# Retention stage of a fused network: head sums on column groups with channels on partitions, products in a buffer of their own, norm scaling on ScalarE, blocks unrolled

## What is computed

```python
def step(carry, xs):
    S, K = carry
    pq, pk, vt, bt, mt = xs        # elu(rope(q))+1, elu(rope(k))+1, v, beta, mix
    K = K * bt[..., None] + pk[:, :, None, :]
    S = S * bt[..., None, None] + pk[:, :, None, :, None] * vt[:, :, None, None, :]
    num = jnp.einsum('bhd,bhmdc->bhmc', pq, S)
    den = jnp.einsum('bhd,bhmd->bhm', pq, K) + EPS
    y = jnp.sum(num / den[..., None] * mt[..., None], axis=2)
    return ((S, K), y)
...
y = jnp.moveaxis(ys, 0, 1).reshape(b, t, H) @ Wout.T + bout
z = x + y                          # here x is the normed input of the stage
mu = z.mean(-1, keepdims=True)
var = ((z - mu) ** 2).mean(-1, keepdims=True)
return (z - mu) / jnp.sqrt(var + LN_EPS) * ln_g + ln_b
```

## Time and profile before

| what | value |
| --- | --- |
| time, median of 3 runs | 2612.34 us (2611.93 to 2614.21) |
| profiled execution, its own time | 2613.99 us |
| span in its trace | 2612.3 us |
| busy over the whole span | PE 84%, DVE 69%, ACT 37%, POOL 20% |
| retention stage in the trace | about 959.5 to 1376 us |
| mean granted TensorE clock, whole span | 0.87 |

### The profile page before, as it was taken

One profiled execution on the slowest core, in us unless ns is written; L12 is line 12 of the kernel. 1 busy time (PEld: TensorE's weight loads), 2 busy tenths in 40 slices (PEclk: granted clock), 3 DMA queues, 4 the chain that ended last, 5 costly groups with the idle time before them and its releaser, 6 DMA issues. The chain is left out here.

```text
span 2612.3 us, 39415 instructions
## 1 busy us (share of the span) xinstructions
PE 2200.8 (84%) x12850; PEld 1667.5 (64%) x12850; DVE 1804.5 (69%) x5506; ACT 967.5 (37%) x1477; POOL 521.4 (20%) x526
## 2 busy tenths in 40 slices
PE   3777589988799987677667997799989999997999
PEld 2555479876688864545556986455555555556888
DVE  4778678863277867987877886666666666646787
ACT  1223034431144431111103443255656565563443
POOL 0000010100010102322311001244343344421000
PEclk8878689996689996666658998799999999997999
DMA  2000010000000000000000000000000000000000
GB/s 83 3 3 3 2 43 0 0 1 0 0 1 1 1 34 1 1 0 0 0 0 1 0 0 1 1 1 1 1 1 1 1 1 1 1 1 5 9 9 13
DMA packets 13993, 14.90 MB, mean 6 GB/s; under 512 B 3924, under 2 KB 11669, under 8 KB 13334
## 3 DMA queue, kind: packets, MB, share of 16 engines
q1 hardware_dynamic: 13846, 13.11, 1.6%
HBM read 10.22 MB, written 2.88 MB: 5 GB/s over the span
## 5 line engine op out<-in xcount | busy, mean ns | idle before, releaser
L2095 DVE TENSOR_REDUCE soft_mx<-psum 128x1 f32<-128x512 f32 (+3 forms) x608 | 381.0, 659 | 226.5 <-PE psum L1973 132.5
L2016 ACT ACTIVATE soft_prob<-psum 128x1024 f32<-128x1024 f32 (+3 forms) x384 | 306.4, 813 | 217.7 <-PE psum L1904 214.7
L1969 PE MATMUL psum<-soft_own,soft_stack 128*128 128x512 f32 (+3 forms) x768 | 248.3, 384 | 26.8 <-DVE soft_mx L2095 24.4
L1904 PE MATMUL psum<-soft_stack,soft_own 128*128 128x512 f32 (+3 forms) x768 | 233.2, 387 | 1.1 <-ACT soft_prob L2016 0.7
L1904 PEld LDWEIGHTS psum<-soft_stack,soft_own 128*128 128x128 f32 x768 | 119.9, 191 | 142.0 <-issue 89.2
L1969 PEld LDWEIGHTS psum<-soft_own,soft_stack 128*128 128x128 f32 x768 | 142.6, 196 | 80.0 <-DVE soft_mx L2095 62.3
L1919 PE MATMUL psum<-soft_prob,soft_v_pad 128*32 128x512 f32 (+3 forms) x1536 | 164.5, 500 | 5.2 <-ACT soft_prob L2016 3.3
L982 DVE SCALAR_TENSOR_TENSOR x<-psum,ffn1b_cw,x 128x128 f32 (+1 forms) x512 | 144.1, 344 | 32.1 <-PE psum L869 23.1
L982 DVE SCALAR_TENSOR_TENSOR x<-psum,ffn1a_cw,x 128x128 f32 (+1 forms) x512 | 144.1, 344 | 32.0 <-PE psum L869 22.8
L982 DVE SCALAR_TENSOR_TENSOR x<-psum,ffn0b_cw,x 128x128 f32 (+1 forms) x512 | 144.1, 344 | 31.8 <-PE psum L869 22.8
L982 DVE SCALAR_TENSOR_TENSOR x<-psum,ffn0a_cw,x 128x128 f32 (+1 forms) x512 | 144.1, 344 | 31.5 <-PE psum L869 22.5
(11 more groups left out here) (440 smaller groups left out, 4367.8 us busy)
## 6 DMA issues: line engine op xcount, KB each, us to landing
s_ffn_w<-in_ffn_w SPq DMA_DIRECT2D x4, 1024.0 KB, 6.0
out_x<-x SPq DMA_DIRECT2D x8, 256.0 KB, 2.3
mamba_coef_dram<-mamba_out_coef SPq DMA_DIRECT2D x8, 96.0 KB, 1.6
s_ret_w<-in_ret_w SPq DMA_DIRECT2D x1, 640.0 KB
s_ret_cos<-in_ret_cos SPq DMA_DIRECT2D x1, 512.0 KB
s_ret_sin<-in_ret_sin SPq DMA_DIRECT2D x1, 512.0 KB
s_mamba_in<-in_mamba_in SPq DMA_DIRECT2D x1, 256.0 KB
s_soft_sel<-in_soft_sel SPq DMA_DIRECT2D x1, 256.0 KB
```

The source lines that it names most:

```text
L1904: ins = pe.matmul(e_ps[:, n % 2, j, low(n):BLK], own[:, u % 3, 2 * pair + j, kt * P:(kt + 1) * P], stack[:, u % HT, qb * BLK + low(n):(qb ...
L1969: ins = pe.matmul(per_head[:, n, :], stack[:, u % HT, i * P:(i + 1) * P], own[:, u % 3, g, half * BLK:half * BLK + width], start=(n == 0), ...
L2016: nc.scalar.activation(prob[:, done % PROBS, :, low(n):BLK], e_ps[:, n % 2, :, low(n):BLK], ACT.Exp, scale=float(HD) ** -0.5).then_inc(exp ...
L2095: nc.vector.tensor_reduce(mx[:, i, half, heads.start:heads.stop], bank[:, 0:width * len(heads)].rearrange("p (g k) -> p g k", k=width), AX ...
```

## The change

The stage's engine lists are rewritten. What differs:

- **Products.** `state` keeps its values, the ten products of a block go to a new buffer `prod` of five planes, all on DVE. The scans of a sequence's second block start from the last column of `state` itself; the carry copy is gone, and so are POOL's products.
- **Head sums.** The head selector is the stationary operand with 32 columns, the product streams. Four such matmuls take the four groups of 32 columns of the array (`tile_position`), and sums come out with channels or heads on partitions. Denominators: 4 matmuls of 128 columns; numerators: 4 of 512 columns, for each decay. The mixture logits are made in the same way.
- **Division.** ACT copies the denominators with the epsilon added and copies the numerators to SBUF. DVE inverts and multiplies by `mix` (`invert`). PE spreads the 128x128 quotients over channels (`spread`, 8 matmuls with a new constant), into the numerators' banks. DVE multiplies (`divide`), one iteration later than before. PE projects the two decays with accumulation, 8 matmuls; the transpose of `y`, its copy and the addition on DVE are gone.
- **Norms.** Both scalings move from DVE to ACT, which takes `rstd` as scale and `-mean*rstd` as bias. DVE negates the means, POOL multiplies them by `rstd`.
- **Ring.** Three PSUM banks in turn for ten products, the two decay projections among them. The order on every engine is new, and all eight blocks are written out.
- `res` keeps four blocks. A new 128x4x128 constant is loaded with the stage's other weights.

```diff
-POOL_STATES = ((1, 2), (1,))
 W_V, W_BETA = 4, 8
-RING = 8
+JOBS = (0, 1, 2, 3, W_BETA, W_BETA + 1, W_V, W_V + 1, W_V + 2, W_V + 3)
+RING_BANKS = 3
+KEPT = 4
...
+            def invert(q):
+                norm.invert(pool, q)
+                pool.wait_ge(norm.rstd_ready, q + 1)
+                nc.gpsimd.tensor_tensor(shift[:, :], norm.mv[:, :, 0], norm.rstd[:, :], ALU.mult).then_inc(shift_ready, 1)
-            def products(q, p, m):
-                pool.wait_ge(carried, DECAYS * q + m + 1)
-                for s in POOL_STATES[m]:
-                    st = state[:, m, s, :]
-                    ins = nc.gpsimd.tensor_tensor(st, st, phi[:, p, 0, :], ALU.mult)
-                ins.then_inc(prod_pool, 1)
...
             def sums(q, m):
-                for j in range(GT):
-                    cols = slice(j * P, (j + 1) * P)
-                    pe.matmul(den_ps[:, m, j, :], state[:, m, 0, cols], w["head_sel"][:, :], start=True, stop=True)
-                    for c in range(HD4):
-                        ins = pe.matmul(num_ps[:, m, j, c, :], state[:, m, 1 + c, cols], w["head_sel"][:, :],
+                pe.wait_ge(den_prod, n + 1)
+                if m == 0:
+                    pe.wait_ge(mix_tanh_done, min(q + 2, BLOCKS))
+                for j in range(GT):
+                    ins = pe.matmul(den_ps[RH * j:RH * (j + 1), m, :], w["head_sel"][:, :], prod[:, 0, j * P:(j + 1) * P],
+                                    start=True, stop=True, skip_group_check=True, tile_position=(0, RH * j))
+                ins.then_inc(den_ready, 1)
+                pe.wait_ge(num_prod, n + 1)
+                for c in range(HD4):
+                    ins = pe.matmul(num_ps[RH * c:RH * (c + 1), m, :], w["head_sel"][:, :], prod[:, 1 + c, :],
+                                    start=True, stop=True, skip_group_check=True, tile_position=(0, RH * c))
+                ins.then_inc(num_ready, 1)
+
+            def spread(q):
+                pe.wait_ge(rd_ready, q + 1)
+                for m in range(DECAYS):
+                    pe.wait_ge(num_copied, DECAYS * q + m + 1)
+                    for j in range(GT):
+                        ins = pe.matmul(num_ps[:, m, j * P:(j + 1) * P], w["spread"][:, j, :], rd[:, m, :],
                                         start=True, stop=True)
+                    ins.then_inc(spread_ready, 1)
...
+            def scale(q):
+                for j in range(GT):
+                    ins = nc.scalar.activation(norm.xn[:, j, :], x[:, q * GT + j, :], ACT.Identity,
+                                               scale=norm.rstd[:, j:j + 1], bias=shift[:, j:j + 1])
+                ins.then_inc(norm.xn_ready, 1)
...
+            for i in range(BLOCKS):
+                if i + 2 < BLOCKS:
+                    scale(i + 2)
+                if i + 1 < BLOCKS:
+                    decays(i + 1)
+                    mixture(i + 1)
+                    exponentials(i + 1)
+                copy_num(i, 0)
+                if i + 2 < BLOCKS:
+                    copy_x(i + 2)
+                if i:
+                    scale_z(i - 1)
+                copy_den(i)
+                copy_num(i, 1)
...
                 for s in range(STATES):
                     ins = nc.vector.tensor_tensor_scan(
                         state[:, m, s, :], beta[:, p, m, :], phi[:, p, 1, :] if s == 0 else kv[:, p, s - 1, :],
-                        0.0 if p == 0 else carry[:, m, s:s + 1], ALU.mult, ALU.add)
+                        state[:, m, s, BLK - 1:BLK] if p else 0.0, ALU.mult, ALU.add)
                 ins.then_inc(scanned, 1)
-                nc.vector.tensor_copy(carry[:, m, :], state[:, m, :, BLK - 1]).then_inc(carried, 1)
                 for s in range(STATES):
-                    if s in POOL_STATES[m]:
-                        continue
-                    st = state[:, m, s, :]
-                    ins = nc.vector.tensor_tensor(st, st, phi[:, p, 0, :], ALU.mult)
+                    ins = nc.vector.tensor_tensor(prod[:, s, :], state[:, m, s, :], phi[:, p, 0, :], ALU.mult)
+                    if s == 0:
+                        ins.then_inc(den_prod, 1)
+                ins.then_inc(num_prod, 1)
...
+            def invert(q):
+                dve.wait_ge(den_copied, q + 1)
+                nc.vector.reciprocal(rd[:, :, :], rd[:, :, :]).then_inc(inverted, 1)
+                dve.wait_ge(mix_ready, q + 1)
+                nc.vector.tensor_tensor(rd[:, :, :], rd[:, :, :], mix[:, q % 2, :, :], ALU.mult).then_inc(rd_ready, 1)
+            def divide(q):
+                for m in range(DECAYS):
+                    dve.wait_ge(spread_ready, DECAYS * q + m + 1)
+                    nc.vector.tensor_tensor(ym[:, m, :], num_ps[:, m, :], num[:, m, :], ALU.mult).then_inc(ym_ready, 1)
```

More of the change, by code:

```diff
@@ new lines, in project @@
+            def project(q):
+                pe.wait_ge(ym_ready, DECAYS * (q + 1))
+                if q:
+                    pe.wait_ge(z_ready, q)
+                for j in range(GT):
+                    for m in range(DECAYS):
+                        ins = pe.matmul(y_ps[:, j, :], ym[:, m, j * P:(j + 1) * P], w["out"][:, :],
+                                        start=(m == 0), stop=(m == DECAYS - 1))
+                ins.then_inc(y_ready, 1)
+            tokens(0)
+            ring(0, range(6))
@@ L1475, in _ @@
+            project(BLOCKS - 1)
         @block.scalar
@@ L1490, in sigmoids, with decays @@
+            def decays(a):
+                for i in range(DECAYS):
+                    act.wait_ge(ring_ready, len(JOBS) * a + 4 + i + 1)
+                    if a:
+                        act.wait_ge(beta_ready, a)
+                    nc.scalar.activation(th[:, i, :], ring_ps[:, (len(JOBS) * a + 4 + i) % RING_BANKS, :], ACT.Tanh,
+                                         bias=half_b[:, i:i + 1], scale=0.5).then_inc(tanh_done, 1)
                 act.wait_ge(tanh_done, DECAYS * (a + 1))
-                if not first:
-                    act.wait_ge(carried, DECAYS * (a - 1))
@@ new lines, in _ @@
+            statistics(0)
+            statistics(1)
+            rope(0)
+            features(0)
+            for i in range(BLOCKS):
+                if i + 2 < BLOCKS:
+                    statistics(i + 2)
+                if i + 1 < BLOCKS:
+                    rope(i + 1)
+                if i:
+                    divide(i - 1)
+                scans(i, 0)
+                if i:
+                    add_residual(i - 1)
+                if i + 1 < BLOCKS:
+                    features(i + 1)
+                scans(i, 1)
+                if i:
+                    finish(i - 1)
+                invert(i)
@@ L1682 @@
+            divide(BLOCKS - 1)
+            add_residual(BLOCKS - 1)
+            finish(BLOCKS - 1)
 HEADS, HD = 16, 8
```

429 lines of the change are left out of this document (192 added, 237 removed).

## The result

The changed kernel took 2530.89 us (median of 4 runs, 2529.36 to 2531.32), the kernel before beside it on the same chip 2613.28 us (4 runs, 2611.93 to 2614.66). The ratio is 0.9684, 95% interval 0.9667 to 0.97. The predicted time was 2526 us. Its profiled execution took 2530.77 us, with a span of 2529.0 us.

The account below looks back on a forecast made before the run. The bound was taken as a cycle in the retention stage: DVE's work plus its waits for PE. Work 280, waits 46 and gaps 6 gave 331 us against 416.5, -85.5, so 2526 us from 2612.34; range 2504 to 2554.

Parts of the forecast that it names:

- rival 5: DVE's products stay at 1.37 us because something other than POOL slowed them: +34, 2560; chance 0.04.
- Collisions: POOL's `keep` beside DVE's scans: two of 1.05 us for six blocks, 12.6 us; 13 in place of 7, +6.
- the fourth rope product behind the spreading: PE makes it after eight spreading matmuls, so DVE waits 2.8 us a block at 1.2 GHz, none at 2.4.
- `kv`: Fourth product waits for one of three PSUM banks: DVE waits 0.9 us a block at 1.2 GHz, none at 2.4.
- Features: PE's and ACT's chain ends at 23.1 us, DVE at 22.4: it waits 0.7 at 1.2 GHz, nothing at 2.4.
- No wait before the reciprocal: At `divide`, the denominators' sums and copy are hidden at both clock levels, so the 33.0 us wait goes.
- Rivals 3 and 4: Column groups run in series: +50, 2577, chance 0.06; with 1.2 GHz for the whole stage too: 2615, chance 0.03.
- The drain at a change of tiling mode: PE changes between full width and four column groups four times a block; softmax shows no gap there.
- ACT's scalings: Norm scalings as 8 ACT instructions of 128x128 a block, 0.39 us at most each, 3.1 us beside DVE's scans.
- A few us either way: The FFN following the retention stage starts at whichever clock level that stage left, shifting time by a few us.
- Rival 1: Lower clock throughout, as PE does fewer matmuls: waits rise by 11, start and end by 5, about 2545; chance 0.14.
- rival 2: Higher clock more often, or fewer collisions: the 22 us of steady waits vanish, 2506; chance 0.13.

Follow-up runs that it names:

- g1_dve_products: Kernel before, with all ten products of a block on DVE, still in place, and POOL's products and their waits gone: 2603.11 us, ratio 0.9959.
- h5_pool_products: Changed kernel with three of the ten products of a block back on POOL, still into the separate buffer: 2538.67 us, ratio 0.9723.
- h6_keep_late: Changed kernel with POOL's `keep` moved behind the power of z and held until the next block's `phi` is made: 2513.54 us, ratio 0.9639.
- h8_double_num: Changed kernel with the four numerator matmuls of each decay made twice, same values over themselves: 2521.79 us, ratio 0.9668.
- g3_unrolled: Kernel before, with the loop over the retention stage's four middle blocks written out, nothing else: 2622.9 us, ratio 1.0043.
- i2_pad: Changed kernel with 40 unused one-element memsets on DVE at the retention stage's start, moving later DVE code: 2512.22 us, ratio 0.9622.
- i1_all: Changed kernel with `keep` released by `phi`, fourth rope product between the two spreadings, and ACT's exponentials ahead of the mixture: 2506.5 us, ratio 0.9597.
- all three edits together: Kernel before, all products on DVE, norm scalings on ACT, head sums of three of four numerator columns left out: 2574.51 us, ratio 0.9858.
- h7_rope_between: Changed kernel with PE's fourth rope product put between the two decays' spreadings, not behind both: 2524.11 us, ratio 0.9671.

## Why the prediction was right, and where it missed

**Time and direction.** 2526 us was predicted, 2530.89 measured, inside the range of 2504 to 2554. The two errors of the sum have opposite signs: the stage came out at 324.5 us where 331 was predicted, 6.5 less, and the rest of the span at 2204.5 in place of 2195.8, 8.7 more where nothing was counted. So the span became 2529.0 in place of 2526.8. That these two nearly cancel is luck; the stage's own error, 2%, is the measure of the forecast.

**DVE's work, 280 us predicted, 277.2 measured.** Products 50.1 and 49.6, right; rival 5 (they stay slow) falls, and g1_dve_products and h5_pool_products show that POOL was the cause. The norm scalings left DVE, right. Collisions: twelve at 1.05, 12.6 us, were put on `keep`; h6_keep_late, which takes `keep` off the scans, gained 12.2. Right, and it was also cheap to remove.

**DVE's waits and gaps, 46 + 6 predicted, 47.3 measured.** By stretch: start 12 predicted and 37.20 - 24.84 = 12.4 measured; end 12 and 10.8; the steady part, 22 and the gaps of 6, came to 24.1. Inside the steady part the forecast had the largest item right, the fourth rope product behind the spreading (2.8 x 0.7 x 7 = 13.7, measured 13.6 with 1.2 of it at the start). `kv` was 7.3, 6.3 without the start, where 0.9 x 0.7 x 7 = 4.4 follows from the walk. Features were 3.4 and measured 1.7, at the start alone. The wait at `ym` was not in the walk: 6.1 us, of which 3.2 belong to the end. The share of the lower clock was taken over from before, 70%; the mean of 0.71 makes it 58%, but the spreading stood in the lower part: 3.78 us in six of eight blocks, where h8_double_num has 2.06 to 3.12. So the total of the steady waits came out nearly right from one item that was right, one too small, one too large and one that was missing.

**No wait before the reciprocal, numerators in 2.1 us at the lower level.** Right: none, and 1.94 us (1.93 or 1.94 in all sixteen sets). Rivals 3 and 4, which needed serial groups, fall. (The forecast says that weights and streams differ by group here as in softmax; here the four groups take the same head selector, and only the streams differ.) All sixteen sets ran at the lower level; of the higher one i1_all shows a single mixed case, 1.27 us.

**The drain at a change of tiling mode.** In h8_double_num the full-width spreading starts at 1163.17, before the modelled end of the groups' matmuls at 1163.24. As in the earlier trace rows, no gap is seen. The Trainium skill, TensorEngine Tiling (Array Packing), Tiling Modes, has a drain there; a cost of 0.2 us or more at this change should have shown as a gap, as far as the modelled end can be trusted.

**ACT's scalings, "0.39 us at most".** Mis-sized: 483 ns. Four of them in order take 1.65 us. DVE waits for them where nothing covers them: 3.2 us at the start of the stage (`n_stats` behind `n_xn`) and 3.1 at its end, each time together with POOL's power.

**"A few us either way" for the rest.** This is the step that missed. The few us came to 8.7, and the reason given, the clock level that the stage leaves to the following FFN, was not it: that FFN took 238.5 us where it took 239.4. The last FFN lost 7.1 us through the place of DVE's code; g3_unrolled and i2_pad show it from both sides. The trace of the kernel before has such pauses in the same place, 2.1 and 2.2 us, so they could have been a term. That all eight blocks are written out was costed at nothing; alone it is worth 0.4% to the worse. The other 3.8 us, in the stages ahead, are within what traces differ by.

**Slips of the working.** 280 + 46 + 6 is 332; 331 was taken. Rival 1's terms (11 and 5 on top of 2526) give 2542 where 2545 is written, and rival 2's give 2504, not 2506. Rival 5 was priced at +34: eighty products of 1.37 us would take 109.6 us, 59.5 more than the 50.1 of the forecast, so about 2586. None of them moves the range, from which rival 5 was left out.

**What the sum hid.** The terms were right for DVE's work in the new kernel; they are not what a part brings alone. Products and collisions were put at -23.5 and +6, and alone gave 13.4 us, since `keep` then cost the scans 11.9. The norms were put at 17.8 and alone gave 3.9. Short sums do not set that free: with all three edits together 40.4 us came, where DVE's lost work (12.1 and 16.8 us) and 26 for the sums would have made 55, because behind the shorter wait at `divide` (7.8 us) DVE waited longer for `kv` and rope, 45.5 us in place of 35.0. The remaining 50.7 came with the new order, the third bank, the new division and the removed small instructions, all at once. A sum by parts holds for the whole change; it does not say what one part would bring.

## What to carry to other kernels

Work taken from an engine counts only where nothing else holds that engine up next: moving 17 us of DVE's work to ACT gained 4 us while 33 us of waiting stood behind it, and shortening that one wait did not change this while the waits at `kv` and rope stayed. When POOL shares SBUF with scans or products on DVE, place POOL's instructions by a semaphore where DVE reads PSUM; that was worth 12.2 us, about as much as moving three of ten products between the two engines (13.4 and 11.4 us), and a single wait did it. And when a change makes one engine's code longer, look at the first instruction behind each loop's jump in unchanged stages.

## What was not expected of the hardware

- More work on PE made a stage shorter by 11.9 us, because PE had no pause before a stretch that DVE waits for, and ran it at 2.4 GHz (0.99) and not at 1.2 (0.50). In the kernel of i1_all the same work brought 1.0 us, no more than traces differ by.
- DVE waits up to 4.7 us (h7_rope_between) at a loop's jump, with nothing to release it in the profile. In the last FFN the two waits are 2.1 and 2.2 us before, 4.6 and 4.5 after, and none with forty more instructions ahead. DMA's share in the first of these stretches is 0.13 in the window from 2346 to 2353 us, against 0.03 over that stage. Which places are bad no run here tells; it stays open.
- A pause of PE of 4.5 us costs more than itself: sixteen records behind it took 3.20 us in place of 1.95, at a granted clock of 0.70.
